# The first group's convolution bias through a DRAM scratch row, with its store and its spread load on ACT's queue

## The reference

```python
# layer 0: grouped convolution, plus a bias for each batch entry and output channel
out = lax.conv_general_dilated(x, weight, window_strides=(1,), padding=[(4, 4)], feature_group_count=4, ...)
ctx = jnp.einsum('nd,od->no', c, c_weight)          # (32, 64)
out = out + ctx[:, :, None] + bias[None, :, None]   # bias is fside_S_0, (64,)
x = x + ffn_with_lora(out)
# layer 1: attention over 8 mixing matrices from the same condition
h = gelu(c @ W0 + b0); h = gelu(h @ W1 + b1)
att = softmax(h @ W2 + b2)                          # (32, 8)
x = x + gated_experts(einsum(att-mixed weights, x) + att @ bias_k)
```

## Time and profile before

| | us |
|---|---|
| median of 3 runs | 658.17 |
| lowest and highest run | 656.51, 658.33 |
| the profiled execution | 656.7 |
| its span | 654.9 |

### The profile page before, as it was taken

The page is one execution under the profiler, slowest core; times in us unless marked ns, Lnnn a source line. Parts: engine busy times, 40 slices in busy tenths (PEclk is TensorE's granted clock), DMA queues, the critical chain, the costliest instruction groups (busy, mean ns, idle before and its releaser), DMA issues.

```text
span 654.9 us, 8354 instructions
## 1 busy us (share of the span) xinstructions
PE 648.1 (99%) x3197; PEld 537.7 (82%) x3197; DVE 451.4 (69%) x690; ACT 214.0 (33%) x275; POOL 73.8 (11%) x91
## 2 busy tenths in 40 slices
PE   9999999999999999999999999999999999999997
PEld 8878888888897788888889788888879888888885
DVE  2859469549377788558769758636967856665785
ACT  2714135233144024335115312333423421433420
POOL 1598200000000160000000042000000000000000
PEclk9999999999999999999999999999999999999999
DMA  8587714986969926776976682287797664037795
GB/s 303 210 293 279 299 50 144 356 246 218 392 228 379 356 100 260 280 223 245 366 275 220 261 318 97 102 225 245 290 325 264 273 248 184 0 118 203 211 345 221
DMA packets 51594, 157.98 MB, mean 241 GB/s; under 512 B 5488, under 2 KB 6384, under 8 KB 51568
## 3 DMA queue, kind: packets, MB, share of 16 engines
q1 hardware_dynamic: 46240, 148.05, 62.7%
q10 hardware_dynamic: 5328, 9.61, 4.8%
HBM read 131.94 MB, written 25.71 MB: 241 GB/s over the span
## 4 chain that ended last, share of the span: by engine, by line
PE 91%; DVE 3%; DMA 3%; issue 1%; SPq 1%; ACT 0%; DVEq 0%
PE bank L1374 25%; PE bank L1376 24%; PE bank L1375 24%; PE bank L1388 9%; PE bank L1408 3%; DMA piece_lo<-kept 2%; PE bank L1395 2%; PE bank L1414 1%; PE bank L1402 1%; PE bank L1400 1%; PE bank L1415 1%; DVE x L925 1%; DMA gate<-hidden_w 1%; DVE u_lo L1012 1%; DVE work L932 1%
## 5 line engine op out<-in xcount | busy, mean ns | idle before, releaser
L893 DVE TENSOR_TENSOR piece_lo<-raw,piece_hi 128x1024 fp32r<-128x1024 f32 x60 | 74.1, 1239 | 90.0 <-ACT piece_hi L647 89.8
L647 ACT ACTIVATE piece_hi<-raw 128x1024 fp32r<-128x1024 f32 x60 | 63.4, 1058 | 147.1 <-PE bank L1376 103.2
L1374 PE MATMUL bank<-piece_hi,u_hi 128*128 128x512 f32 x272 | 107.9, 397 | 0.0
L1376 PE MATMUL bank<-piece_hi,u_lo 128*128 128x512 f32 x272 | 107.3, 395 | 0.0
L1375 PE MATMUL bank<-piece_lo,u_hi 128*128 128x512 f32 x272 | 107.3, 394 | 0.0
L1374 PE MATMUL bank<-v_hi,piece_hi 128*128 128x512 f32 x256 | 101.8, 398 | 0.0
L1376 PE MATMUL bank<-v_hi,piece_lo 128*128 128x512 f32 x256 | 101.1, 395 | 0.0
L1375 PE MATMUL bank<-v_lo,piece_hi 128*128 128x512 f32 x256 | 101.0, 394 | 0.0
L1374 PE MATMUL bank<-piece_hi,v_hi 128*128 128x512 f32 x192 | 76.0, 396 | 0.8 <-DMA piece_lo<-kept 0.8
L1376 PE MATMUL bank<-piece_hi,v_lo 128*128 128x512 f32 x192 | 75.8, 395 | 0.0
L1375 PE MATMUL bank<-piece_lo,v_hi 128*128 128x512 f32 x192 | 75.8, 395 | 0.0
(11 more groups left out here) (143 smaller groups left out, 800.7 us busy)
## 6 DMA issues: line engine op xcount, KB each, us to landing
raw<-pieces SPq DMA_DIRECT2D x76, 512.0 KB, 5.5
piece_hi<-kept SPq DMA_DIRECT2D x48, 512.0 KB, 4.7
piece_lo<-kept SPq DMA_DIRECT2D x48, 512.0 KB, 5.8
x<-x SPq DMA_DIRECT2D x16, 512.0 KB, 5.3
gate_x<-gates ACTq DMA_DIRECT2D x32, 256.0 KB
out<-x SPq DMA_DIRECT2D x32, 256.0 KB, 4.8
conv_in<-conv_x SPq DMA_DIRECT2D x15, 516.0 KB, 7.1
conv_in<-pieces SPq DMA_DIRECT2D x12, 512.0 KB, 8.8
```

Of the source, the lines that this page charges most:

```text
L647: act.activation(piece_hi[:, n % SLOTS, :], raw[:, r % RAWS, :], ACT.Copy).then_inc(s_piece_hi, 1)
L893: dve.tensor_tensor(piece_lo[:, n % SLOTS, :], raw[:, r % RAWS, :], piece_hi[:, n % SLOTS, :].bitcast(F32), ALU.subtract).then_inc(s_piece ...
L1374: pe.matmul(to, left_hi, right_hi, start=first, stop=False)
L1376: return pe.matmul(to, left_lo, right_hi, start=False, stop=last)
```

## The change

The matmul of ones, the diagonals and the copy by ACT go. `context()` on PE becomes the product for all 32 entries, right behind convolution 0, and DVE only copies it to `biases`. On ACT the store of `biases` moves ahead of `hidden(0)`; `spread_first()` waits until the store has landed and issues a load that spreads the first 512 numbers over 128 partitions. DVE's first `conv_item` waits for that load. SP's wait for the matmul of ones ahead of the loads of x goes.

```diff
@@ -417,7 +414,6 @@
                 next_raw(5)
                 sp.wait_ge(s_const_hi, 4)
                 sp.wait_ge(s_const_lo, 3)
-                sp.wait_ge(s_p_ctx_bc, 1)
                 for h in range(2):
                     for th in range(2):
                         load_x(0, th, h)
@@ -718,9 +714,9 @@
                     act.activation(hid[:, n, :], banks[0][:, 0:NB], ACT.Gelu, bias=(b0s, b1s)[n]).then_inc(s_hid, 1)
 
                 def spread_first():
-                    act.wait_ge(s_p_ctx_bc, 1)
-                    act.activation(cond_bc[:, :, :].rearrange("p b c -> p (b c)"), banks[1][:, :],
-                                   ACT.Copy).then_inc(s_ctx_bc, 1)
+                    act.wait_ge(s_out_ctx, 16)
+                    act.dma_start(cond_bc[:, :, :].rearrange("p b c -> p (b c)"),
+                                  spread[0:1, 0:GB * C].to_broadcast([P, GB * C])).then_inc(s_ctx_bc, 16)
 
                 def biases_out(n, ready, step, done):
                     act.wait_ge(ready, step)
@@ -753,14 +749,13 @@
                         piece_used(act, n - SLOTS)
                     act.activation(piece_hi[:, n % SLOTS, :], raw_first(n), ACT.Copy).then_inc(s_piece_hi, 1)
 
+                biases_out(0, s_ctx, 1, s_out_ctx)
                 hidden(0)
                 spread_first()
                 for b in range(GB):
                     conv_hi(0, b)
                     if b == 0:
                         hidden(1)
-                    if b == 2:
-                        biases_out(0, s_ctx, 3, s_out_ctx)
                     if b == 3:
                         split_first(0)
                     if b == 4:
@@ -1014,16 +1009,7 @@
 
             def first_group():
                 def context():
-                    dve.wait_ge(s_first, 16)
                     dve.wait_ge(s_p_ctx, 1)
-                    dve.tensor_scalar(ctx_t[0:C, :], banks[3][0:C, 0:GB], fs[0:C], None, ALU.add).then_inc(s_ctx, 1)
-                    dve.wait_ge(s_ctx, 1)
-
-                    dve.tensor_tensor(diag, ident[0:C, None, 0:C].to_broadcast([C, GB, C]),
-                                      ctx_t[0:C, :, None].to_broadcast([C, GB, C]), ALU.mult).then_inc(s_ctx, 1)
-
-                def rest_of_context():
-                    dve.wait_ge(s_p_ctx, 2)
                     dve.tensor_copy(biases[:, 0, :], banks[2][0:NB, 0:C]).then_inc(s_ctx, 1)
 
                 def softmax_max():
@@ -1071,12 +1057,10 @@
 
                     dve.wait_ge(s_conv, b + 1)
                     if b == 0:
-                        dve.wait_ge(s_ctx_bc, 1)
+                        dve.wait_ge(s_ctx_bc, 16)
                     conv_item(b, 4 + b % 4)
                     if b:
                         conv_lo(0, b - 1)
-                    if b == 1:
-                        rest_of_context()
                     if b == 4:
                         split_first(0)
                     if b == 5:
@@ -1441,7 +1425,9 @@
             def first_group():
                 def context():
                     pe.wait_ge(s_first, 16)
-                    pe.matmul(banks[3][0:C, 0:GB], cw_t, cond_t[:, 0:GB], start=True, stop=True).then_inc(s_p_ctx, 1)
+                    pe.matmul(banks[2][0:NB, 0:C], cond_t, cw_t, start=True, stop=False)
+                    pe.matmul(banks[2][0:NB, 0:C], ones[0:1, 0:NB], frow[0:1, :], start=False,
+                              stop=True).then_inc(s_p_ctx, 1)
 
                 def hidden(n):
                     if n == 0:
@@ -1451,14 +1437,9 @@
                     pe.matmul(banks[0][:, 0:NB], (w0s, w1s)[n], (cond_t, hid[:, 0, :])[n], start=True,
                               stop=True).then_inc(s_p_hid, 1)
 
-                def rest_of_context():
-                    pe.matmul(banks[2][0:NB, 0:C], cond_t, cw_t, start=True, stop=False)
-                    pe.matmul(banks[2][0:NB, 0:C], ones[0:1, 0:NB], frow[0:1, :], start=False,
-                              stop=True).then_inc(s_p_ctx, 1)
-
                 def logits():
                     pe.wait_ge(s_hid, 2)
-                    pe.wait_ge(s_ctx, 3)
+                    pe.wait_ge(s_ctx, 1)
                     pe.matmul(banks[2][0:NB, 0:KC], hid[:, 1, :], w2s, start=True, stop=False)
                     pe.matmul(banks[2][0:NB, 0:KC], ones[0:1, 0:NB], b2s[0:1, :], start=False,
                               stop=True).then_inc(s_p_logit, 1)
@@ -1527,17 +1508,11 @@
                     if b == 0:
                         context()
                         hidden(0)
-                    if b == 1:
-                        pe.wait_ge(s_ctx, 2)
-                        pe.matmul(banks[1][:, :], ones[0:C, :], diag.rearrange("p b c -> p (b c)"), start=True,
-                                  stop=True).then_inc(s_p_ctx_bc, 1)
-                        rest_of_context()
                     if b == 2:
                         hidden(1)
                     if b == 5:
                         logits()
 
-                pe.wait_ge(s_ctx_bc, 1)
                 pe.wait_ge(s_att_exp, 1)
                 ffn_piece(0)
                 mix_weights()
```

More of the change, by code:

```diff
@@ L120, in adaln_ffn_kernel @@
         hid = sb("hid", [P, 2, NB])
-        ctx_t = sb("ctx_t", [P, GB])
         biases = sb("biases", [NB, 2, C])
@@ L149, in adaln_ffn_kernel @@
         lora_b_stage = x1[:, 1, :]
-        diag = x1[0:C, 2, 0:GB * C].rearrange("p (b c) -> p b c", b=GB)
         banks = [ctx.enter_context(nc.psum_tensor(f"bank{i}", [P, HALF], F32)) for i in range(8)]
@@ L166, in adaln_ffn_kernel @@
         s_p_logit = sem("s_p_logit")
-        s_p_ctx_bc = sem("s_p_ctx_bc")
         s_p_att = sem("s_p_att")
```

## The result

The changed kernel takes 664.47 us (median of 6 runs, 663.65 to 666.59), the kernel before on the same chips 657.61 us: 6.9 us more, a ratio of 1.0112 with a 95% interval of 1.0093 to 1.0132. The forecast was 663.9 us and slower. The profiled execution took 664.7 us, with a span of 662.9.

The account below looks back on a forecast made before the run. PE, busy 648.1 of 654.9 us, was taken as the bound, so a late start goes through. Bias arrival 6.7 us later less 0.97 given back makes 5.7; 658.17 + 5.7 = 663.9 us, range 660.3 to 668.3.

Parts of the forecast that it names:

- The mechanism and the sign: First group: DVE waits for the bias by way of DRAM, PE stands 5.2 us; slower by over 0.3%, chance 0.91.
- PE's pair ends at 8.80, store issued at 9.2: Start: the pair of lines 1455 and 1456 ends at 8.80 us, DVE copies by 9.15, ACT issues the store at 9.2.
- The store, 5.5 us: ACT's 8 KB store of `biases` to DRAM: 5.5 us, between like stores of 4.9 and 6.0, landing at 14.7.
- The load, 4.7 us: 256 KB spread load into 128 partitions on ACT's queue: 4.7 us as in the nearest row, landing at 19.4.
- The rival of the long load: Spread load queues behind SP's loads, 7.7 us; bias lands at 22.9, shift 9.2 us, 667.4 us; chance 0.17.
- The pace, 0.97 us given back: DVE's first-group items: two waits for PE (0.84 us) and the copy's 0.13 vanish, giving back 0.97 us.
- the rival of the slow PE: PE slow for two convolutions after its 5.2 us gap: 0.9 us more, 664.8 us; chance 0.14.
- No second wait before the first piece: Before the first weight piece: PE should wait 1.9 us for ACT's exponentials; no such wait would show the forecast wrong.
- PE's busy time up, not down: Whole kernel: PE's busy time was to fall by some 1.3 us, the work taken from it.
- Everything behind moves together: After the first weight piece: every later row stays at a constant distance of 5 to 6 us.
- arrival: Bias reaching DVE: its first item starts at 19.5 in place of 12.80 us, 6.7 us later.
- The rival of short transfers: Store and load pass SP's queue quickly; bias lands at 15.2, shift 1.5 us, 659.7 us; chance 0.09.

Follow-up runs that it names:

- the early order: The kernel before with only the product, DVE's copy and ACT's store moved early, bias still by the matmul of ones: 656.44 us, repeated at 657.36.
- first experiment: The changed kernel with the two products taken from PE put back as dead work between convolutions 1 and 2: 664.94 us, ratio 1.0121.
- the second trace: The changed kernel unaltered, measured and traced once more: 665.32 us, ratio 1.0107 to the kernel before.
- The quiet queue: The changed kernel with SP's loads from the first weight piece on held back until the spread load landed: 661.23 us, ratio 1.0053.
- the gap filled: The changed kernel with 27 unread matmuls of ones on PE before convolution 4: 666.67 us, ratio 1.0135; with 21, 667.18 us.
- the pure delay: The kernel before with 28 matmuls of ones on PE right ahead of the first weight piece: 665.89 us, ratio 1.014.

## Why the prediction was right, and where it was off

**The mechanism and the sign: right.** DVE's first item waits for a DMA, PE stands 5.17 us before convolution 4 with DVE as releaser (forecast 5.2), and the early order by itself costs nothing. PE's saved work is worth nothing (first experiment).

**PE's pair ends at 8.80, store issued at 9.2: 9.75 and 10.11.** PE waited 1.4 us for `taps` in this execution. In the second trace the store went out at 9.65. Off by 0.4 to 0.9 us, by how the first loads land.

**The store, 5.5 us: 0.3 us too long, and 0.5 to 1.0 in the other traces.** 5.2 in the first trace, 4.5 to 5.0 in those of the kernels that share it. That gave back part of what the late issue cost.

**The load, 4.7 us: too low.** It was 4.7 in the first trace, but 6.6, 6.7, 7.0 and 6.6 in the four others on ACT's queue. I chose it because the row of 4.7 was on ACT's queue, and held the 7.7 of SP's queue to be another case. Neither the queue nor the mean DMA share would have given the right row. The row of 4.7 ran at a share of 0.81; here the first trace's load of 4.7 ran at 0.82 and the second's of 6.7 at 0.76. The quiet queue shows only that far less company makes the load shorter (3.4 at 0.31). The longer loads go with a later end of SP's own loads, 21.5 us and after against 19.7; what makes those land later in one execution than in another stays open. The rival of the long load was priced at 7.7 and had the right direction: typical is something between, and that term of the sum was about 2 us short in most executions.

**The pace, 0.97 us given back: 0.8 and 0.3 us in the two traces of the changed kernel, 1.2 us with the clock held up.** DVE had a third wait for PE from 8 to 28 us, of 0.39 us at 22.41, which the prediction doesn't count. It stands behind the step on which the exponentials hang and changes nothing in the sum. Here the rival of the slow PE came true beside the forecast. I had given it 0.14, at 0.9 us. The price was right (0.4 to 0.9 us in three of the four traces with an unfilled gap of 5 us and more, nothing in the fourth), the chance too low. The Trainium skill's "TensorE: Matmul & The Clock Gate", Part 1, which I had set beside it, says that an idle array falls to 1.2 GHz; the traces agree for gaps of 5.0 to 7.1 us. I should have given the rule more weight than the lack of such a gap in the trace of before.

**No second wait before the first piece, and PE's busy time up, not down.** The prediction names the missing wait as a sign of being wrong, since it puts the bound on PE's own convolutions, and there it was. Both follow in the main from the clock: two convolutions of 5.96 us filled the 1.9 us of waiting that I had forecast, and 1.3 us of work less became 1.1 us more (649.2 against 648.1). With the gap filled, the forecast wait for ACT is there (1.55 us).

**"Everything behind moves together": wrong.** This is the step that failed. A first delay of 6.5 us became 8.0 at the second group, and the pure delay shows the same without the change. My ground was that PE waits only 1.3 us behind the first 9 us of the trace. That shows that nothing absorbs a delay. It doesn't show that nothing adds to it: DVE's and ACT's chains over the gates and the second group's first items ran close behind PE, and a row without a wait doesn't say how close.

**The sum.** Forecast 5.7 us, measured 6.9. In the first trace: arrival +7.29 in place of 6.7, given back 0.77 in place of 0.97, second loss 1.5 in place of 0, makes 8.0 for that execution, whose time is 8.0 us above that of the traced execution before. The two medians lie only 6.9 apart, because the traced execution before (656.7) is faster than the kernel's median (657.6): part of what I call the second loss comes in some executions of the kernel before too, 0.9 us in its second trace. That 663.9 is so near 664.47 is luck in part. The median that I added the shift to was 658.17, of three runs, and that of six runs is 657.61, which hides 0.6 of the 1.2 us by which the shift was short; and the first trace happened to have the load of 4.7. The rival of short transfers is out: in the changed kernel the store and the load took 9.9 to 11.5 us together.

## What to carry to other kernels

A small value that every partition needs within a few microseconds should not go by way of DRAM at a time when another queue keeps the DMA engines full: the store and the load took 2.7 and 3.4 us at DMA shares of 0.23 and 0.31, and 4.5 to 5.2 and 4.7 to 7.0 us with SP's loads beside them, and a matmul of 1.1 us plus a copy of 0.6 did the same job. Price such a DMA by a range and not by its nearest row: rows alike in queue, size and mean DMA share lay at 4.7 and at 6.7 us. And where an engine is 99% busy, read how close the other chains run behind it before taking a delay at one for one: a delay of 6.6 us on PE alone cost 8.7.

## What the hardware showed that I had not expected

- Two loads of 256 KB issued 0.07 us apart took 11.0 us on SP's full queue and 6.1 on ACT's. Issued at 14.4 to 15.4 us, with 4.4 to 8.4 us of SP's loads still to come, the spread load took 6.9 on SP's queue and 4.7 to 7.0 on ACT's.
- A gap of 1.98 us on PE, behind 4.9 us of matmuls of ones, was followed by a granted clock of 0.50 (24 to 26 us), and one of 2.54 us in the quiet queue's trace too (30 to 32 us), while gaps of 1.86 and 1.46 us behind convolutions were not. One trace each, so this tells nothing of where the border lies.
- The same pair of convolutions took 3.8 us at 1.00, and 5.19 to 6.45 us behind a gap at a low clock, as the clock came back sooner or later.
- Being late by 1.8 us and by 8.4 us gave nearly the same second loss, 1.4 and 1.8 us. Its cause stays open.
- The same stretch of DMA issues came in two forms in the unchanged kernel: SP's store in 2.9 us and ACT's three loads in 2.9, or 0.4 and 4.0.
